# Expert results laid out by token position, read back in 4 KB runs, and the last sum split in halves

## The reference

```
h = conv_block(x, ...)                      # embedding, layer norm, gated convolution, layer norm
h = h + attention(layernorm(h), Wq, Wk, Wv)
h = h + ffn(layernorm(h), Wr, br, W1, b1, W2, b2)

def ffn(x, ...):                            # T = 16 * 128 tokens of 128 values
    probs = softmax(x @ Wr + br)            # 16 experts
    topk_w, topk_idx = top_k(probs, 2)      # weights divided by their sum
    for e in range(16):
        o = gelu(x @ W1[e] + b1[e]) @ W2[e] + b2[e]
        y += combine[:, e:e+1] * o          # combine: topk_w where expert e was chosen, else 0
    return x + y
```

## Time and profile before

| | us |
|---|---|
| median of 3 runs | 245.03 |
| lowest and highest run | 244.9 and 247.89 |
| span of the profiled execution, first to last instruction | 229.0 |
| what lies around the span, if the profiled execution took the median | 16.0 |
| DVE busy, share of the span | 122.7, 54% |
| POOL busy, share of the span | 100.8, 44% |
| ACT busy, share of the span | 94.2, 41% |
| PE busy, share of the span | 163.2, 71% |

### The profile page before, as it was taken

How to read it: one execution, slowest core, us unless ns; L and a number is a source line. 1 busy time by engine, 2 the same in 40 slices (tenths; PEclk the granted TensorE clock), 3 DMA queues, 4 the chain that set the end, 5 groups by cost and what they waited for, 6 DMA issues and landing times.

```text
span 229.0 us, 3461 instructions
## 1 busy us (share of the span) xinstructions
PE 163.2 (71%) x833; PEld 111.6 (49%) x833; DVE 122.7 (54%) x511; ACT 94.2 (41%) x256; POOL 100.8 (44%) x158
## 2 busy tenths in 40 slices
PE   4859769886989579608926274899999999991000
PEld 1634434563466266405504131588888888870000
DVE  2531356279587863796562762245555566550174
ACT  2131252525560651145123003467777777760240
POOL 5000520502220672057257472057777777777060
PEclk9999967999799965955785569599999999999555
DMA  1799920000000010001001152234344442100576
GB/s 55 225 340 320 410 88 0 4 0 0 1 3 1 12 59 24 0 12 61 24 24 62 49 177 83 59 89 115 106 119 109 121 112 63 20 17 12 150 217 183
DMA packets 23148, 20.18 MB, mean 88 GB/s; under 512 B 3107, under 2 KB 20813, under 8 KB 22874
## 3 DMA queue, kind: packets, MB, share of 16 engines
q1 hardware_dynamic: 19418, 15.16, 22.5%
q0 software_dynamic: 2560, 4.27, 5.7%
q10 hardware_dynamic: 1152, 0.54, 0.8%
HBM read 13.49 MB, written 7.51 MB: 92 GB/s over the span
## 4 chain that ended last, share of the span: by engine, by line
PE 60%; DVE 14%; ACT 7%; DMA 6%; POOL 6%; issue 5%; SPq 1%; DVEq 0%; POOLq 0%; ACTq 0%
PE bank L979 10%; PE bank L995 9%; PE bank L862 9%; PE bank L986 5%; PE bank L831 4%; DVE stats L597 3%; POOL slots L431 3%; PE bank L934 3%; PE bank L899 3%; PE bank L974 3%; DMA work_b<-parts 2%; PE bank L900 2%; PE bank L902 2%; ACT stage L475 2%; PE bank L842 2%
## 5 line engine op out<-in xcount | busy, mean ns | idle before, releaser
L444 POOL DMA_INDIRECT parts<-work_a,xt x48 | 47.2, 983 | 25.8 <-DVE work_a L770 15.8
L431 POOL DMA_INDIRECT slots<-stage,slot_of x32 | 31.6, 987 | 17.8 <-issue 8.9
L862 PE MATMUL bank<-x1T,convw_sb 128*128 128x512 f32 x48 | 29.2, 756 | 2.5 <-ACT x1T L486 2.5
L979 PE MATMUL bank<-w_sb,xtT 128*128 (+1 forms) x96 | 30.1, 396 | 0.0
L995 PE MATMUL bank<-w_sb,act_hT 128*128 (+1 forms) x192 | 29.8, 278 | 0.0
L764 DVE TENSOR_TENSOR hid<-bank,fb_bc 128x256 f32<-128x256 f32 x48 | 20.4, 425 | 13.3 <-PE bank L979 7.7
L995 PEld LDWEIGHTS bank<-w_sb,act_hT 128*128 128x128 f32 x192 | 25.7, 194 | 0.2 <-ACT act_hT L552 0.2
L770 DVE TENSOR_TENSOR work_a<-bank,fb_bc 128x128 f32<-128x128 f32 x48 | 14.0, 292 | 19.3 <-PE bank L995 19.3
L542 ACT ACTIVATE xtT<-bank 128x128 f32<-128x128 f32 x48 | 13.3, 278 | 20.2 <-PE bank L974 20.2
L420 POOL TENSOR_TENSOR work_c<-work_b,g_bc 128x256 f32<-128x256 f32 x8 | 5.7, 723 | 34.9 <-ACT work_b L475 34.9
L986 PE MATMUL bank<-ident,act_h 128*128 128x128 f32 x96 | 19.4, 284 | 0.3 <-ACT act_h L547 0.3
(11 more groups left out here) (160 smaller groups left out, 272.6 us busy)
## 6 DMA issues: line engine op xcount, KB each, us to landing
xt<-slots SPq DMA_DIRECT2D x48, 66.0 KB, 1.8
w_sb<-in_L_ffn_W_dram SPq DMA_DIRECT2D x1, 2048.0 KB, 9.5
fb_bc<-in_L_ffn_b_dram SPq DMA_DIRECT2D x1, 2048.0 KB, 18.6
fb_bc<-in_L_ffn_b_dram SPq DMA_DIRECT2D x1, 1024.0 KB, 11.2
work_b<-parts SPq DMA_DIRECT2D x4, 256.0 KB, 3.9
work_a<-parts SPq DMA_DIRECT2D x4, 256.0 KB, 5.6
out_dram<-work_c SPq DMA_DIRECT2D x4, 256.0 KB, 2.4
parts<-work_a,xt POOLq DMA_INDIRECT x48, 2.3
```

The lines of the kernel that those rows point to most:

```text
L431: pool.indirect_dma_start(out=slots, out_offset=bass.IndirectOffsetOnAxis(ap=slot_of[:, g, k, s:s + 1].bitcast(U32), axis=0), in_=stage[:, ...
L444: pool.indirect_dma_start(out=parts, out_offset=bass.IndirectOffsetOnAxis(ap=xt[:, u, ROW_PLACE:ROW_PLACE + 1].bitcast(U32), axis=0), in_= ...
L862: last = pe.matmul(by_seq(acc[:]), convw_sb[:, w, half * D:(half + 1) * D], x1T[:, g, :, w:w + L], start=(w == 0), stop=(w == TAPS - 1))
L979: pe.matmul(bank[2 + b][:, 0:HID], xtT[:, b, :], flat(w1_sb[:, expert_of(j), :]), start=True, stop=True).then_inc(t_h_psum, 1)
```

## The change

In `parts` a row is now numbered position, sequence, choice. The 8 rows that a partition needs for a group (4 sequences, 2 choices) are one run of 4 KB, and 128 such runs, 16 KB apart, make one load of 512 KB. There are four loads in place of eight. Groups 0 and 1 land in `work_a`, groups 2 and 3 in `work_b`. The iota that writes the places has other steps, but the same number of elements; the scatters are the same instructions with other places.

ACT and POOL now take two blocks of each group instead of three (MANY = 2). DVE takes the other two: for these it does both operations, and it goes through each group as a whole before it begins the next: two operations on the second choice, two on the first choice that wait for them, then the wait for POOL, then the other two on the first choice. DVE thus has 6 operations a group, 24 in all, in place of 20.

```diff
+        part_rows = parts.rearrange("(p b k) d -> p b k d", b=SEQS, k=TOPK)
+        halves = GROUPS // 2
+        got = [(work_a, work_b)[g // halves][:].rearrange("p g n -> p (g n)")
+               .rearrange("p (h b k d) -> p h b k d", h=halves, b=GS, k=TOPK)[:, g % halves] for g in range(GROUPS)]
...
+        MANY = GS // 2
...
-            both = parts.rearrange("(k b p) d -> k p b d", k=TOPK, p=P)
-            for k, buf in ((1, work_b), (0, work_a)):
-                for g in range(GROUPS):
-                    sp.dma_start(by_seq(buf[:, g, :]), both[k, :, g * GS:(g + 1) * GS, :]).then_inc(parts_in[k][g], 16)
+            for g in range(GROUPS):
+                sp.dma_start(got[g], part_rows[:, g * GS:(g + 1) * GS]).then_inc(parts_in[g], 16)
...
                 pool.iota(stage[:, k, :, :, ROW_PLACE:ROW_PLACE + 1].bitcast(I32),
-                          pattern=[[N, GROUPS], [P, GS], [0, 1]], base=k * T, channel_multiplier=1)
+                          pattern=[[GS * TOPK, GROUPS], [TOPK, GS], [0, 1]], base=k, channel_multiplier=SEQS * TOPK)
...
-                most = slice(0, (GS - 1) * P)
+                most = slice(0, MANY * P)
                 pool.tensor_tensor(work_d[:, g, most], work_c[:, g, most], h0[:, g, most], ALU.add).then_inc(summed, 1)
...
-                act.wait_ge(parts_in[1][g], 16)
-                for s in range(GS - 1):
-                    last = act.activation(blocks(work_c[:, g, :], s), blocks(work_b[:, g, :], s), ACT.Identity,
+                act.wait_ge(parts_in[g], 16)
+                for s in range(MANY):
+                    last = act.activation(blocks(work_c[:, g, :], s), got[g][:, s, 1, :], ACT.Identity,
                                           scale=w_top[:, g * GS + s, 1:2])
...
+            def first_choice(g, s):
+                return dve.scalar_tensor_tensor(
+                    out=blocks(work_c[:, g, :], s), in0=got[g][:, s, 0, :], scalar=w_top[:, g * GS + s, 0:1],
+                    in1=blocks(work_d[:, g, :], s), op0=ALU.mult, op1=ALU.add)
+
             for g in range(GROUPS):
-                dve.wait_ge(parts_in[1][g], 16)
-                last = dve.scalar_tensor_tensor(
-                    out=blocks(work_d[:, g, :], GS - 1), in0=blocks(work_b[:, g, :], GS - 1),
-                    scalar=w_top[:, g * GS + GS - 1, 1:2], in1=blocks(h0[:, g, :], GS - 1), op0=ALU.mult, op1=ALU.add)
-            link(last)
-            for g in range(GROUPS):
-                dve.wait_ge(parts_in[0][g], 16)
+                dve.wait_ge(parts_in[g], 16)
+                made = [mark(dve.scalar_tensor_tensor(
+                    out=blocks(work_d[:, g, :], s), in0=got[g][:, s, 1, :], scalar=w_top[:, g * GS + s, 1:2],
+                    in1=blocks(h0[:, g, :], s), op0=ALU.mult, op1=ALU.add)) for s in range(MANY, GS)]
+                for s in range(MANY, GS):
+                    dve.wait_ge(dve_chain, made[s - MANY])
+                    first_choice(g, s)
                 dve.wait_ge(summed, g + 1)
-                for s in range(GS):
-                    last = dve.scalar_tensor_tensor(
-                        out=blocks(work_c[:, g, :], s), in0=blocks(work_a[:, g, :], s), scalar=w_top[:, g * GS + s, 0:1],
-                        in1=blocks(work_d[:, g, :], s), op0=ALU.mult, op1=ALU.add)
+                for s in range(MANY):
+                    last = first_choice(g, s)
                 last.then_inc(y_out, 1)
```

More of the change, by code:

```diff
@@ L163, in tower_kernel @@
         act_hT = sb("act_hT", [P, 2, HID])
+        part_rows = parts.rearrange("(p b k) d -> p b k d", b=SEQS, k=TOPK)
+        halves = GROUPS // 2
+        got = [(work_a, work_b)[g // halves][:].rearrange("p g n -> p (g n)")
+               .rearrange("p (h b k d) -> p h b k d", h=halves, b=GS, k=TOPK)[:, g % halves] for g in range(GROUPS)]
+        token_rows = out.rearrange("b t d -> t b d")
         y_sb = work_a[:].rearrange("p g (s d) -> p (g s) d", d=D)
@@ L193, in tower_kernel @@
             sem, ("t_xT_psum", "t_xT", "t_h_psum", "t_h", "t_act", "t_actT_psum", "t_actT", "t_y_psum", "t_y"))
-        parts_in = [[sem(f"parts{k}_in{g}") for g in range(GROUPS)] for k in range(TOPK)]
+        parts_in = [sem(f"parts_in{g}") for g in range(GROUPS)]
         base_ready, stored, scaled_y, summed, y_out = map(sem, ("base_ready", "stored", "scaled_y", "summed", "y_out"))
@@ L356, in _ @@
                 sp.wait_ge(placed[u], 16 * (TILES // U))
-            both = parts.rearrange("(k b p) d -> k p b d", k=TOPK, p=P)
-            for k, buf in ((1, work_b), (0, work_a)):
-                for g in range(GROUPS):
-                    sp.dma_start(by_seq(buf[:, g, :]), both[k, :, g * GS:(g + 1) * GS, :]).then_inc(parts_in[k][g], 16)
-            tokens = out.rearrange("b t d -> t b d")
+            for g in range(GROUPS):
+                sp.dma_start(got[g], part_rows[:, g * GS:(g + 1) * GS]).then_inc(parts_in[g], 16)
             for g in range(GROUPS):
                 sp.wait_ge(y_out, g + 1)
-                sp.dma_start(tokens[:, g * GS:(g + 1) * GS, :],
-                             by_seq(work_c[:, g, :])).then_inc(stored, 16)
+                sp.dma_start(token_rows[:, g * GS:(g + 1) * GS, :], by_seq(work_c[:, g, :])).then_inc(stored, 16)
             sp.wait_ge(stored, 16 * GROUPS)
```

## The result

| | before | after |
|---|---|---|
| median of 12 runs each, same chips | 246.36 us | 247.08 us |
| lowest and highest | 243.01 and 249.97 | 245.07 and 250.16 |
| ratio, 95% interval | | 1.0091, 1.0049 to 1.0133 |
| time of the profiled execution, and its span | not listed, 229.0 | 246.94, 245.2 |

The change costs 0.9%, or 2.2 us (1.2 to 3.3), in this comparison; later ones gave 0.4 to 0.6%. The forecast was 0.8 us faster.

The account below looks back on a forecast made before the run. Bound: first load's landing, then DVE and POOL work whose times add. Landing 216.70 + first group 2.35 + three groups 6.13 ends DVE at 225.2, not 225.97; with 3.0 store and 16.0 around the span, 244.2 us, range 242.6 to 246.8.

Parts of the forecast that it names:

- its first part: End of the program: chain of waits runs through the fourth second-choice load, then DVE to 225.97, then 3.0 us of store.
- the store behind it keeps its 3.0 us: After DVE's last operation: the last store and the span's end stay 3.0 us behind DVE, giving span 228.2.
- First landing: First of the four loads: lands at 216.70 against 216.22 before, + 0.69 for size and - 0.21 for faster bytes.
- DVE, ACT, POOL: Final sum: 24 DVE operations over 8.5 us, 0.47 per POOL add, ACT 0.69 a group; DVE ends at 225.2.
- Rate and size: Loads of the final sum: 4 KB packets at 380 GB/s (ends 273 and 400), landings 1.38 us apart.
- rival 3: Loads: they still go in 512-byte pieces, both sides being given as four dimensions; 244.7 us, chance 0.14.
- rival 2: Loads: rows 16 KB apart are read slowly, at 180 GB/s; + 3.4 us, 248.4 us, chance 0.10.
- Rivals 1 and 4: Final sum: DVE and POOL dearer, 246.4 us, chance 0.22; POOL's adds in DVE's gaps cost 0.1, 243.1 us, 0.12.
- within 2%: Whole kernel: measured time differs by less than 2%, 4.9 us, from before; chance 0.92.
- Time around the span: Outside the profiled span: the runs' median lies 16.0 us above it, so span 228.2 becomes 244.2.

Follow-up runs that it names:

- the late memset: Kernel before plus a POOL memset of 16 columns at its end that waits for DVE's last result; ratio 1.0177 (1.0125 to 1.0230).

## Why the prediction was wrong

**The step that failed** is in its first part: "Behind that come the last store, issued at 226.00 with 2.4 us to its landing, and the end of the span at 229.0: 3.0 us after DVE", and with it "the store behind it keeps its 3.0 us". SP is through with the store 2.53 us after DVE (15.15 less 12.62), and what made 3.0 of it was POOL's DRAIN. So the end before had two paths: POOL's, and the store's 0.3 us ahead of it in that profile and level with it in the two later ones. The prediction saw only the store's. By the store's path the changed kernel's tail is as long as before (SP's DRAIN 15.15, 14.92, 15.18 before; 14.99 to 15.25 after). By POOL's path it is 0.7 to 0.8 longer, since POOL's last add used to wait for the fourth of eight loads and now waits for the last of four. The prediction had the numbers for POOL's last add: its fourth landing 7.5 after the issue, 0.69 for ACT, 0.08, 0.72 for the add make 9.0, where the changed kernel had 9.2 to 9.5 and before 8.3 to 8.8. With 6.6 for the DRAIN and 0.2 behind it, its own numbers give an end at 15.8, no earlier than before (15.65): none of the 0.8 us would have arrived.

**First landing:** mis-sized, the second failed step. DVE's start was forecast at 3.4 after the issue and measured at 3.96 to 4.25. The term was "262 KB more: + 0.262 / 380 GB/s = 0.69; its first 262 KB move faster than at about 290: - 0.21". The new loads move at 147 to 303 GB/s in their first microsecond and a half, and reach 380 and more only behind the first load. So the first 262 KB were not faster; at equal size, in 2 KB runs, they landed 0.4 later. These 0.6 to 0.9 us are why DVE's end stayed where it was (12.5 to 12.8) in place of 0.8 earlier; they alone would have made it no change.

**DVE, ACT, POOL:** right. Stretch of DVE 8.5, measured 8.52 to 8.58; an add's price to DVE 0.47, measured about 0.49 for each of the three that lie on its work; it waits for POOL once, in the first group (0.6), and for no load after that. The adds lie earlier than forecast, one in group 0 and two in group 1, which leaves the sum as it is.

**Rate and size:** right. The kernel's packets fell from 23148 to 19500, by the 3584 that 512 packets of 4 KB save against 4096 of 512 bytes (and 64), so rival 3 is out; rates of 350 to 430 GB/s after the first 3 us and the run with new places only rule out rival 2. Landings came 1.2 to 1.35 apart, forecast 1.38. Rivals 1 and 4 are out by the stretch and by the three long operations. That the change would stay within 2% came true.

**Time around the span:** wrong. I took 16.0; it is 1.7, and the other 14 us were the difference between two kinds of chip. The predicted time rested on a median from another kind of chip than the span. Its base moved too: the median of before was 245.03 in 3 runs and 246.36 in 12. Of the 2.9 us between 244.2 and 247.08 that is 1.3; the other 1.6 are the 0.8 that did not come and the 0.8 by which the tail grew.

**How much is shown.** The tail is 0.76 us longer in the mean of four profiles against three (16.18 less 15.42), or 0.31%. That POOL's end carries it is shown by the late memset and by the kernels without POOL. The ratios show it less well. If the 0.36% that the kernel before showed against itself, twice, is an offset of the comparison, 1.0067 is expected; the four ratios were 1.0091, 1.0037, 1.0047 and 1.0064. But the run with new places only, at 0.9998, had no such offset, and on the one chip with both, the kernel before run again and the changed kernel came out alike (1.0040 and 1.0047). Taken alone the first ratio asks for 2.2 us, 1.4 more than the tail explains. That rest was not settled.

## What to carry to other kernels

Before an edit near a program's end, look at the last DRAIN of every engine, and not only at the chain of waits: an engine that has long finished can hold the end. Here leaving the helper with the long DRAIN out of the last stage won more than its help; giving it only the early groups shortened the tail but showed no gain in time. When a load is made bigger, count who waits for its first byte and who for its last: doubling the load put the first landing 1 us later, whatever the runs, while 4 KB runs brought the last landing 1.6 us forward. And compare stages from event to event, since a span and a median may come from different chips.

## What the runs showed of the hardware

POOL's final DRAIN ends 6.6 us after the end of POOL's last operation (6.58 to 6.68 by the rounded rows), in all 20 profiles: after adds of 2, 256 or 384 columns, after a memset of 0.11 us, and after a scatter (in the kernels without POOL in the sum). What it does in this time, no run shows.

A first load in 2 KB runs landed 0.4 us later than one of the same 256 KB in 512-byte runs (3.47 against 3.03 on one chip, 3.39 on another), though the longer runs are the faster ones once the stream runs. For first loads of 512 KB the run's length made no difference (4.13 in 512-byte runs, 3.96 to 4.25 in 4 KB runs).

On some chips the expert part has pauses, after every third tile at first and later after every fourth or fifth. ACT and DVE are idle for 1.4 and 2.0 us while PE goes on; when they resume PE runs out of work for 1.1 us. From the first scatter of `parts` to the last it took 75.3 to 76.7 us there, against 60.6 to 61.1 on the others, and the spans were 245 to 250 against 226 to 230 (without the late memset). The clock granted in that part is 1.00 on both. The cause stays open, and so does whether it is the chip or the time.
